# A fused vision-tower kernel: the fp16 cast of the gelu output moves to ScalarE, VectorE's routing chain runs three links to a gelu step, and the expert counts get another PSUM bank

## The reference, cut to what matters

```python
# MLP of the attention layer (D = 256, FF = 1024)
h2 = _ln(x, g2, beta2)
x = x + (jax.nn.gelu(h2 @ w1 + b1, approximate=False) @ w2 + b2)
...
# routing of the mixture layer: 8 experts, top 4, capacity 1280 of T = 8192 tokens
mult, sel = _sparse_mixer(dyn_logits)
...
mask_dyn = (rw > 0).astype(jnp.int32)
mask_dyn = mask_dyn * (jnp.cumsum(mask_dyn, axis=0) <= cap)
...
gw = jax.nn.softmax(jnp.where(expert_mask == 0, -jnp.inf, full_logits), axis=-1)
# shared expert: silu(x @ gate) * (x @ up), then down, weighted by gw's last column
```

## Time and profile before

| | |
|---|---|
| median of 3 executions | 2729.38 us (2725.92 to 2731.68) |
| the profiled execution, its own time | 2748.85 us |
| its span, first to last instruction | 2747.1 us |
| `mlp_phase`, bodies 1 to 15 | from 1670 us to 2503 us of the span |
| TensorE busy over the span | 2405.4 us (88%) |
| VectorE busy over the span | 1892.2 us (69%) |
| ScalarE busy over the span | 1462.3 us (53%) |
| GpSimd busy over the span | 1566.7 us (57%) |

### The profile page before, as it was taken

The page is one execution under the profiler, slowest core; times in us unless marked ns, Lnnn a source line. Parts: engine busy times, 40 slices in busy tenths (PEclk is TensorE's granted clock), DMA queues, the critical chain, the costliest instruction groups (busy, mean ns, idle before and its releaser), DMA issues. The chain is left out here.

```text
span 2747.1 us, 61186 instructions
## 1 busy us (share of the span) xinstructions
PE 2405.4 (88%) x22832; PEld 1738.9 (63%) x22832; DVE 1892.2 (69%) x4174; ACT 1462.3 (53%) x2731; POOL 1566.7 (57%) x1546
## 2 busy tenths in 40 slices
PE   4799999999999999999999858898888898986564
PEld 3588788888888888888887724444444444443453
DVE  2577777777777777777777736787777777865342
ACT  3466666666666666666666534434443444432232
POOL 1465656565665656565656522665566556655576
PEclk8999999999999999999999979999999999998887
DMA  4111111111121111111110020121121111100675
GB/s 146 43 61 63 41 60 61 60 44 60 60 64 40 44 40 44 36 48 36 44 40 13 10 98 24 64 72 51 47 69 67 50 41 49 36 20 9 143 137 79
DMA packets 115060, 152.21 MB, mean 55 GB/s; under 512 B 16537, under 2 KB 75917, under 8 KB 114768
## 3 DMA queue, kind: packets, MB, share of 16 engines
q1 hardware_dynamic: 88880, 124.46, 14.1%
q0 software_dynamic: 23808, 21.74, 4.5%
q10 hardware_dynamic: 2080, 2.10, 0.2%
HBM read 81.71 MB, written 90.96 MB: 63 GB/s over the span
## 5 line engine op out<-in xcount | busy, mean ns | idle before, releaser
L952 POOL TENSOR_TENSOR qkl<-fz,qkh 128x512 f16<-128x512 f32 x256 | 307.6, 1201 | 309.5 <-DVE qkh L849 305.2
L1817 POOL DMA_INDIRECT slot_dram<-xt,slot_u x256 | 257.6, 1006 | 74.6 <-issue 73.6
L521 PE MATMUL pF<-nh,qk_h 128*128 128x256 f16 x1024 | 282.0, 275 | 8.1 <-DVE nl L836 4.4
L522 PE MATMUL pF<-nh,qk_l 128*128 128x256 f16 x1024 | 281.2, 275 | 0.0
L523 PE MATMUL pF<-nl,qk_h 128*128 128x256 f16 x1024 | 281.2, 275 | 0.0
L964 POOL TENSOR_TENSOR ol<-on,oh 128x256 f16<-128x256 f32 x256 | 171.8, 671 | 153.5 <-ACT oh L786 153.5
L971 POOL TENSOR_TENSOR kvl<-kvacc,kvh 128x260 f16<-128x260 f32 x192 | 150.2, 782 | 107.8 <-ACT kvh L794 107.8
L1797 POOL TENSOR_TENSOR al<-az,ah 128x512 f16<-128x512 f32 x64 | 79.2, 1238 | 220.9 <-DVE ah L1586 220.9
L763 ACT ACTIVATE sh<-sm 128x512 f16<-128x512 f32 x256 | 159.3, 622 | 84.6 <-DVE sm L872 84.6
L846 DVE SCALAR_TENSOR_TENSOR fz<-pF,ez 128x512 f32<-128x512 f32 x256 | 175.3, 685 | 31.9 <-ACT ez L746 29.8
L740 ACT ACTIVATE rz<-pF 128x512 f32<-128x512 f32 x256 | 150.7, 589 | 86.0 <-PE pF L523 81.4
(11 more groups left out here) (313 smaller groups left out, 8577.0 us busy)
## 6 DMA issues: line engine op xcount, KB each, us to landing
xs<-in_x SPq DMA_DIRECT2D x128, 256.0 KB, 2.6
slot_dram<-blank SPq DMA_DIRECT2D x8, 1360.0 KB, 6.0
xg<-slot_dram SPq DMA_DIRECT2D x40, 272.0 KB, 3.2
h_dram<-hT SPq DMA_DIRECT2D x32, 256.0 KB, 2.1
x_dram<-x SPq DMA_DIRECT2D x32, 256.0 KB, 2.1
at_dram<-at SPq DMA_DIRECT2D x32, 256.0 KB, 2.2
x0b<-x_dram SPq DMA_DIRECT2D x16, 512.0 KB
atb<-at_dram SPq DMA_DIRECT2D x16, 512.0 KB
```

The lines of the kernel that those rows point to most:

```text
L521: pe.matmul(out, wh, mh, start=first, stop=False, skip_group_check=True)
L522: pe.matmul(out, wl, mh, start=False, stop=False, skip_group_check=True)
L952: nc.gpsimd.tensor_tensor(qkl[:, pair:pair + 2, cols], fz[:, n % 2, :, :], qkh[:, pair:pair + 2, cols], ALU.subtract).then_inc(fl_ready, 1)
L1817: nc.gpsimd.indirect_dma_start(io["slot_dram"], bass.IndirectOffsetOnAxis(slot_u[:, c, k:k + 1], 0), xt[:, i % 2, c, :], None, bounds_chec ...
```

## The change

`w1` on ScalarE casts `gz` to `gh` itself behind each gelu, with a wait for that gelu. `w1` on VectorE no longer casts and runs three links in each step instead of two, so that `mask` keeps links 27 and 28 only. The counts go to columns 64 to 103 of `pL`. The waits follow the banks: the counts wait for the logits to have been read, `mean3` for the counts to have been read, and `var2` no longer waits for the counts.

```diff
             def var2(i):
                 if not (type(i) is int and i < 2):
-                    pe.wait_ge(cum_read, count(i, 1, -1))
+                    pe.wait_ge(ht_ready, count(i, 2, -2))
...
             def mean3(i, before):
                 if before:
                     pe.wait_ge(lg_ready, count(i, 1, 0))
+                    pe.wait_ge(cum_read, count(i, 1, 0))
...
             def gate_up(i, after, js):
                     else:
                         pe.wait_ge(ht_ready, count(i, 2, 2))
-                        pe.wait_ge(cum_read, count(i, 1, 1))
...
             def counts(i):
                 pe.wait_ge(mask_ready, count(i, 1, 1))
-                pe.wait_ge(ht_ready, count(i, 2, 2))
+                pe.wait_ge(lg_ready, count(i, 1, 1))
                 first = True
                 for c in range(CH + 1):
-                    out = pA[1][:, c * EXPERTS:(c + 1) * EXPERTS]
+                    out = pL[:, COUNTS + c * EXPERTS:COUNTS + (c + 1) * EXPERTS]
...
             # ScalarE, w1, behind the gelu of step j
+                    act.wait_ge(gz_ready, count(i, FT, j + 1))
+                    if j == 0 and not at_start(i):
+                        act.wait_ge(w2_done, count(i, 1, 0))
+                    nc.scalar.activation(gh[:, j, :], gz[:, j % 4, :], ACT.Copy).then_inc(gh_ready, 1)
...
             # VectorE
             def w1(i, before, js):
-                if js[0] == 0 and not at_start(i):
-                    ve.wait_ge(w2_done, count(i, 1, 0))
                 for j in js:
                     ve.wait_ge(gz_ready, count(i, FT, j + 1))
-                    nc.vector.tensor_copy(gh[:, j, :], gz[:, j % 4, :]).then_inc(gh_ready, 1)
-
                     if j % 2 == 1:
                         ve.wait_ge(gh_ready, count(i, FT, j + 1))
                         nc.vector.tensor_tensor(gl[:, j, :], gz[:, j % 4, :], gh[:, j, :], ALU.subtract).then_inc(gl_odd, 1)
                     if before:
-                        routing(i - 1, EXP1_AFTER + 2 * j, EXP1_AFTER + 2 * j + 2)
+                        routing(i - 1, EXP1_AFTER + 3 * j, EXP1_AFTER + 3 * j + 3)
...
             # links 29 and 30 read pL[:, COUNTS:...] in place of pA[1]
             def mask(i):
-                routing(i, EXP1_AFTER + (0 if type(i) is int and i == SEQS - 1 else 2 * FT), MASK_AFTER)
+                routing(i, EXP1_AFTER + (0 if type(i) is int and i == SEQS - 1 else 3 * FT), MASK_AFTER)
...
+COUNTS = 64
```

More of the change, by code:

```diff
@@ L1690, in routing @@
                 wait(cum_done, 1, 1)
-                link(lambda: V.tensor_tensor(t1[:, :, :], pA[1][:, 0:CH * E].rearrange("p (c e) -> p c e", c=CH),
+                link(lambda: V.tensor_tensor(t1[:, :, :], pL[:, COUNTS:COUNTS + CH * E].rearrange("p (c e) -> p c e", c=CH),
                                              carry[:, :].unsqueeze(1).broadcast_to([P, CH, E]), ALU.add))
-                link(lambda: V.tensor_tensor(carry[:, :], carry[:, :], pA[1][:, CH * E:(CH + 1) * E], ALU.add))
+                link(lambda: V.tensor_tensor(carry[:, :], carry[:, :], pL[:, COUNTS + CH * E:COUNTS + (CH + 1) * E], ALU.add))
                 if lo < state[0] <= hi:
```

## The result

The changed kernel takes 2685.89 us, the median of four runs (2680.65 to 2689.13), against 2729.41 us before in the same runs: a ratio of 0.984, with a 95% interval of 0.9823 to 0.9857. It is 43.5 us faster, where 50.4 us were forecast.

The account below looks back on a forecast made before the run. VectorE's late `m16` stalls TensorE, elsewhere the bound, and slows its clock. Path 3.6 instead of 7.62 us: 4.0 us over 12 bodies, 48, plus 2 (body 9) and 0.3 (body 1): 2729.4 - 50 = 2679 us, range 2670 to 2700.

Parts of the forecast that it names:

- the sign that was named for it, 0.3 us: TensorE, steady body: the counts start within 0.3 us of the last matmul of `w2`(0..6) if the prediction is right.
- "On time within 0.1 us": `m16` on VectorE: ready at 1963.6, where TensorE can take it at 1963.64; 0.1 us a body was allowed.
- 17.3 + 0.45: VectorE up to `m16`: 20.5 us shrinks to 17.3 without the casts, plus 0.45 us waiting for ScalarE's `gh`.
- the 4.5 that the prediction let stay: VectorE: blocking by GpSimd's four `gl`, 4.5 us or so a body, all stays and moves from casts to links.
- as it was read from body 1: TensorE's path from `w2`(0..6) to `gate_up`: body 1's 3.75 us without its 0.35 us of idling, 3.40 us.
- next in line: VectorE after the counts: `hp`, its halves and `tn` end about 1970.5, just before the silu lets `az` start at 1970.7.
- The rival built on it: VectorE blocked 1.57 us at each of four `gl`, `m16` 1.8 us later: 2690 to 2700 us; chance 0.15.
- The step was put at 1.23 to 1.34 us: ScalarE's gelu plus cast: 1.34 us, or 1.23 with overlap, against TensorE's 1.29; 0.1 us a body was allowed.
- The rival's own figures: ScalarE becomes the bound through table loads: steps of 3.9 us, 21 us a body, near 3060 us; chance 0.04.
- the whole second payment: TensorE after the pause: six `w2`(7) matmuls take 2.52 us, 0.42 each instead of 0.216, at 1.2 GHz.
- The fast bound: If blocking vanished with the casts: 4.1 us a body and body 9 in full, 57 us, giving 2672 us.
- the worth of the bank: TensorE's `var2` no longer waiting for VectorE's reading of the counts: worth 0 to 0.5 us, counted as 0.

Follow-up runs that it names:

- four links first: The changed kernel with four links instead of three at gelu step 0, leaving only link 28 in `mask`: 2713.41 us, ratio 0.9889.
- the second cast: The changed kernel with a second, useless cast into a scratch tile in each gelu step on ScalarE: 2765.19 us, ratio 1.0062.
- before's repetition: The kernel before, unchanged, profiled a second time: 2735.76 us in one run, beside a median of 2747.81 us of the same kernel.
- two and four additions: The changed kernel with two, or four, useless VectorE adds ahead of the last links of `mask`: 2737.56 and 2738.70 us, beside 2747.73 of before.
- after and of its repetition: The changed kernel, and the same kernel unchanged in a batch of its own: 2683.77 us, ratio 0.9836, beside 2727.86 us of before.

## Why the prediction was right, and where its sizes were off

**VectorE was late for TensorE, and the pause went.** Right. The pause of the counts fell from 2.75 to 0.53 us in body 6, though the sign that was named for it, 0.3 us, was missed. Neither half does it: `m16` is ready at 23.10 with the cast alone, 23.74 with the links alone, 21.70 with both. An early `m16` is not enough, however: with the old bank it is as early and the gain is only 24 us, and with four links first it is at 21.80 and the bodies take 52.7 us. The whole gain needs the counts to be read soon as well.

**"On time within 0.1 us" is the term that was mis-sized.** VectorE's stretch from the first link to the end of `m16` was put at 17.3 + 0.45 = 17.75 us; it is 1943.65 - 1925.27 = 18.38 us. Of these 0.63 us, to a few hundredths, the wait for `gh`(1) is 0.14 (0.59 for 0.45), the lock 0.3 (4.8 for the 4.5 that the prediction let stay), and the last cast L1688 0.22 (0.40 for 0.18). So the counts wait 0.53 us, where 0.1 was in the sum: 0.43 us a body. The rest of the path came as it was read from body 1, 3.37 us against 3.40, and so did the way from `az` to the logits (1972.34 - 1950.54 = 21.80 us). VectorE's chain is next in line, as was said: its 6.0 us from L1691, in the kernels where it is the limit, would allow `az` 0.3 us sooner than the silu does.

**The lock.** That the blocking belongs to GpSimd's four subtractions and moves to links is shown from both sides: with them, the four links above; without them, none, though the scatters go on. The Trainium skill (SBUF — State Buffer, "Who interferes with whom") agrees here in that an instruction of VectorE waits until GpSimd's ends. It says that whoever issues first gets the pair for the whole instruction; L1663 is recorded 0.39 us ahead of GpSimd's subtraction and still waited, so at that fineness either the records of GpSimd or the rule is rough. The rival built on it (1.57 us for each) took 0.3 us of the 1.8 it might have.

**ScalarE.** The step was put at 1.23 to 1.34 us and is 1.24; `w1` ends 0.09 us later, as forecast, and the second cast shows the rule behind it. (The rival's own figures do not follow that rule: with steps of 3.9 us it gives 6 x 2.61 = 15.7 us a body and 2980 us, not 21 and 3060.) The Trainium skill (ScalarE: Activation LUTs, "Table sets: the hidden batching unit") has it that copy is in every table set; the trace agrees, with one load ahead of the gelus of a body and none among them.

**The clock.** Shown: pauses of up to 1.69 us ahead of the counts are never followed by half the clock; those of 2.06 to 2.78 us are in all but three bodies. These are body 2 of before's repetition (2.34 us) and bodies 10 and 13 of the links alone (2.57 and 2.18 us). What decides between them is open. The prediction read the slow `w2`(7) as the whole second payment. In before it is about half: counts to `gate_up` is 4.87 us at half clock in body 6, 4.14 us at full clock in body 2 of the repetition, where `var2` waits for the late reading instead, and 3.37 us in the kernel after, which has neither.

**The sum.** A steady body gives 7.62 - 3.90 = 3.72 us on TensorE's path, less 0.09 for ScalarE, so 3.63 us (3.65 by the length of body 6) in place of 4.0. Over the twelve bodies of the earlier trace rows that is 4 us less than 48, and 46 in all with what was given to bodies 1 and 9. The medians say 43.5. That the two are so near is in part luck, for the other terms are not what the profiles show. Bodies 1, 9, 14 and 15 gave 1.8, 6.5, 5.5 and 11.4 us between the first profiles, and 0.9, 6.2, 5.5 and 8.4 us between the second profile of each kernel, where 0.3, 2, 4 and nothing were put. Body 0, also put at nothing, is 3.05 us longer in both profiles of the kernel after: from its first matmul of `w1` to its logits it takes 51.25 and 51.27 us, against 48.20 and 48.22 before; I did not follow up why. The profiled executions are 68.2 and 53.5 us apart, the medians 43.5 and 44.1, and no profile of a median run was taken, so it is open where they differ. The fast bound does not add up either: with body 9 as one more body of 4.1 us, 13 of them and 0.3 us for body 1 are 53.6 us, not 57.

**What stays open: the lag.** It is 0.54 us in body 1 of every kernel, where there are no scatters; 1.65 in the steady bodies of before and of its repetition, and 4.5 in body 9; 0.54 in all bodies of after and of its repetition; 1.0 to 4.2 in the steady bodies of every other kernel with scatters under way. Three things are shown. It does not follow the counts: L1691 stands at 25.6 in before, with links alone, and with two and four additions, whether the counts start at 23.9 or 22.5. It goes with the scatters: in the kernel with all `gl` on VectorE it is gone when they are over, and in most bodies ScalarE's gelus are late while they are issued. ScalarE is late in body 15 of before too, with waits of 1.2 to 1.7 us for "remote" among six scatters; there the last matmul of `w1` starts at 18.35, against 10.63 in the kernel after: 7.7 of the 11.4 us that body 15 gave. And it costs: with two and four additions, a second cast or four links first, VectorE's chain from L1691 to `az` (6.0 us) and not TensorE sets the body, and in the old bank `var2` waits as well.

What is not shown is why the kernel after has none. It has its scatters under way when the counts are read: the last of body 6 is issued at 23.28, both with the old bank (lag 2.26) and the new. The bank is no answer by itself, since kernels with the new bank lag too. Nor can the batch be excluded: the variants ran where before took 2745 to 2748 us, after where it took 2728 to 2729. Against the batch speaks that before itself lags by 1.65 us in both. The prediction took before's 1.65 us as part of one stall that body 1's figures replace; that came true, without being explained. For the same reason the worth of the bank, which the prediction put at nothing, isn't known. By the trace of the kernel after L1695 ends at 1944.67 + 0.19, before `w2`(7) does at 1945.36, so a wait there would have cost nothing; by the runs the kernel that differs from it in the bank alone has steady bodies 1.1 to 4.2 us longer and a ratio of 0.9907 instead of 0.984.

## What to carry to other kernels

Before a task is taken off a late engine, ask what its other neighbours do in the time that it frees: the cast alone brought the mask 0.7 us earlier, the order alone 0.1, the two together 2.1, since the freed time fills with waits and held-up links unless enough independent work stands behind it. In time they gave 0.3%, nothing, and together 0.9% with the old bank and 1.6% with the new. A body of the same kernel that lacks one disturbance is a good price list; here it gave the path to 0.03 us. A pause of the matrix engine is worth more than its length when the matmuls behind it run at half the clock. And a variant that should differ in one small thing can differ in another (here how late a result is taken up), so read the body of each before its time is believed.

## What the hardware did unexpectedly

- While indirect scatters were being issued, VectorE and ScalarE took up TensorE's results late in all kernels but the one after: 1.0 to 4.5 us from the counts to L1691 against 0.54 us without scatters, and up to 6 us for gelus when sixteen scatters followed one another. In the kernel after it was 0.54 us with scatters under way. The profile names "remote" as what ended some of these waits.
- A link of 128x32, 0.19 us alone, took 1.2 to 1.8 us against a GpSimd subtraction of 1.2 us when scatters stood between the subtractions; in body 1, without scatters, four operations lost 0.9, 0.9, 1.0 and 0.6 us.
- Removing a wait of 0.59 us on VectorE moved `m16` by 0.1 us in the wrong direction, because the next subtraction then met GpSimd's.
- The same program had medians of 2729 and 2748 us in different batches, with bodies 6 to 8 at the same 54.6 to 54.7 us in both profiles.
- Of two pauses of 2.57 us in the kernel with links alone, one was followed by half the clock and the other by full clock (granted clock of the windows 0.76 and 1.00).
